# Scores from two fp32r parts in 64-row tiles, two heads at a time, and the weighing of a step in two halves

## The reference

```python
x = attention(ln32(x, ln1), ln32(x, ln1), Wq1, Wkv1, Wo1, bo1) + x   # 16 heads, 16 of q and k per head
x = attention(ln32(x, ln2), context, Wq2, Wkv2, Wo2, bo2) + x
x = geglu_ff(ln32(x, ln3), Wff1, bff1, Wff2, bff2) + x
# then one attention of a single head over the context, a residual and an RMS norm
```

## Time and profile before

| | |
|---|---|
| median of three runs | 856.02 us (854.88 to 858.06) |
| span of the profiled execution | 851.5 us; no other time of that execution is given |
| TensorE busy | 732.0 us, 86%, granted clock 0.945 of 2.4 GHz on average |
| VectorE busy | 575.9 us, 68% |
| ScalarE busy | 471.2 us, 55% |
| POOL busy | 70.4 us, 8% |
| DMA | 49.70 MB, 36645 packets |

### The profile page before, as it was taken

One profiled execution on the slowest core, in us unless ns is written; L12 is line 12 of the kernel. 1 busy time (PEld: TensorE's weight loads), 2 busy tenths in 40 slices (PEclk: granted clock), 3 DMA queues, 4 the chain that ended last, 5 costly groups with the idle time before them and its releaser, 6 DMA issues.

```text
span 851.5 us, 12530 instructions
## 1 busy us (share of the span) xinstructions
PE 732.0 (86%) x4064; PEld 365.9 (43%) x4064; DVE 575.9 (68%) x1030; ACT 471.2 (55%) x918; POOL 70.4 (8%) x63
## 2 busy tenths in 40 slices
PE   0885979999999999999999996647788899999991
PEld 0552522222222222222222343423454688888881
DVE  7783958888888787878888363735557595343357
ACT  0451327777777777777777863025556533332265
POOL 8311100000000000000000020320001011000003
PEclk9998969999999999999999999668889999999995
DMA  8165760030303012030300002222210000000002
GB/s 273 62 219 178 181 246 1 13 89 2 96 3 78 22 40 60 1 99 1 87 14 1 2 19 87 78 78 79 76 39 2 1 1 1 1 1 1 1 1 99
DMA packets 36645, 49.70 MB, mean 58 GB/s; under 512 B 4792, under 2 KB 29688, under 8 KB 35576
## 3 DMA queue, kind: packets, MB, share of 16 engines
q1 hardware_dynamic: 36216, 48.65, 19.0%
q0 software_dynamic: 384, 0.47, 0.3%
HBM read 32.76 MB, written 15.97 MB: 57 GB/s over the span
## 4 chain that ended last, share of the span: by engine, by line
PE 61%; DMA 13%; DVE 9%; SPq 7%; ACT 5%; issue 4%; ACTq 0%; DVEq 0%
PE ps L797 12%; PE ps L784 12%; PE ps L659 10%; SPq L398 6%; DMA stack<-mT 5%; DMA stack<-q_parts 4%; PE ps L958 4%; PE ps L959 3%; PE ps L960 3%; PE ps L633 3%; DMA k_parts<-probs 2%; PE ps L752 2%; PE ps L619 2%; PE ps L974 2%; PE ps L973 1%
## 5 line engine op out<-in xcount | busy, mean ns | idle before, releaser
L1441 DVE TENSOR_REDUCE mm<-ps 128x1 f32<-128x1024 f32 x256 | 301.8, 1219 | 75.5 <-PE ps L659 74.4
L1166 ACT ACTIVATE probs<-ps 128x512 f32<-128x512 f32 x512 | 282.3, 597 | 105.6 <-PE ps L784 102.2
L784 PE MATMUL ps<-stack 99*128 99x512 bf16 x512 | 178.9, 388 | 10.5 <-ACT probs L1166 5.8
L659 PE MATMUL ps<-stack 96*128 96x512 bf16 x512 | 156.5, 386 | 14.6 <-DMA stack<-q_parts 11.7
L797 PE MATMUL ps<-probs,v 128*32 128x512 f32 x1024 | 137.2, 608 | 0.0
L784 PEld LDWEIGHTS ps<-stack 99*128 99x128 bf16 x512 | 42.5, 97 | 191.4 <-ACT probs L1166 173.6
L659 PEld LDWEIGHTS ps<-stack 96*128 96x128 bf16 x512 | 48.7, 99 | 70.9 <-DVE mm L1441 17.7
L551 POOL TENSOR_TENSOR x<-x,rows 128x1024 f32<-128x1024 f32 x12 | 28.3, 2360 | 614.6 <-DVE tok L1411 614.6
L1678 DVE SCALAR_TENSOR_TENSOR k<-ps,cols,early 128x512 f32<-128x512 f32 x32 | 24.0, 750 | 70.1 <-PE ps L960 65.8
L1292 ACT ACTIVATE early<-ps,cols 128x512 f32<-128x512 f32 x32 | 22.1, 690 | 88.3 <-PE ps L960 88.3
L1237 ACT ACTIVATE probs<-ps 96x512 f32<-96x512 f32 x64 | 37.2, 595 | 41.7 <-PE ps L883 41.4
(11 more groups left out here) (142 smaller groups left out, 924.3 us busy)
## 6 DMA issues: line engine op xcount, KB each, us to landing
stack<-q_parts SPq DMA_DIRECT2D x32, 192.0 KB
v_groups<-early SPq DMA_DIRECT2D x8, 512.0 KB, 4.4
stack<-q_parts SPq DMA_DIRECT2D x32, 128.0 KB
v<-v_groups SPq DMA_DIRECT2D x8, 512.0 KB, 13.2
q_parts<-probs SPq DMA_DIRECT2D x8, 384.0 KB, 4.4
k_parts<-probs SPq DMA_DIRECT2D x8, 384.0 KB, 3.0
stack<-k_parts SPq DMA_DIRECT2D x8, 384.0 KB, 4.7
q_parts<-early SPq DMA_DIRECT2D x8, 384.0 KB, 2.6
```

The costliest lines, as they stand in the source:

```text
L659: mm_ = eng.matmul(ps[:, 2 * i + kh, :], qs[0:ROWS, slot, half, h, P * (t0 + i):P * (t0 + i) + P], stack[0:ROWS, 2 + slot, h, BLK * kh:BLK ...
L784: eng.matmul(ps[:, st_bank(g, k, h), :], stack[0:KROWS, 2 + slot, h, P * kc:P * kc + P], qs[0:KROWS, slot, half, h, :], start=True, stop=T ...
L1166: eng.activation(probs[:, k % 2, h, :], ps[:, st_bank(g, k, h), :], ACT.Exp, scale=SCALE).then_inc(exp_done, 1)
L1441: eng.tensor_reduce(mm[:, half, k:k + 1], ps[:, 2 * i:2 * i + 2, :], AX.XY, ALU.max).then_inc(s_red, 1)
```

## The change

Scores come from two fp32r parts instead of three bf16 parts: three products (hi x hi, lo x hi, hi x lo), 3 x 16 = 48 rows, and two more rows for the maximum's two parts. Two heads lie above each other in the two 64-row halves of the array (`HT = 2` tiles, `HP = 2` heads in each). Parts are 4 bytes wide instead of 2, two instead of three; the ring has 4 slots. `middle` and `low` are gone, as are two of four steps of `split_max`. The weighing of a step is issued as two halves of 256 columns. The first score tile of a pair lies in rows 64 and up, the second in rows 0 and up. The heads of a step are taken in the order 0, 2, 1, 3, where 0 and 1 lie in the lower tile and 2 and 3 in the upper. In cross-attention two query tiles of four heads are computed into two banks and reduced by one instruction.

```diff
-PARTS = 3
-RING = 5
-ROWS = 6 * DH
+TILE_ROWS, HT = 64, 2
+HP = HG // HT
+PARTS = 2
+RING = 4
+ROWS = 3 * DH
-Q_PART = (0, 0, 0, 1, 1, 2)
-K_PART = (0, 1, 2, 0, 1, 0)
-RUNS = PARTS
+Q_RUNS = ((0, 2), (2, 1))
+K_RUNS = ((0, 1), (1, 2))
+RUNS = HT * len(Q_RUNS)
+HEADS = (0, 2, 1, 3)
...
-        stack = sb("stack", [P, 4, HG, S], BF16)
+        stack = sb("stack", [P, 4, HP, S], F32R)
...
-            def load_stack(dst, src, heads, which, done):
-
-                i = 0
-                while i < PAIRS:
-                    rise = int(i + 1 < PAIRS and which[i + 1] > which[i])
-                    n = 1
-                    while i + n < PAIRS and which[i + n] == which[i] + rise * n:
-                        n += 1
-                    rows = src[which[i]:which[i] + (n if rise else 1)].rearrange("i (r h) n -> (i r) h n", r=DH)
-                    rows = rows[:, heads, :].rearrange("r h n -> r (h n)")
-                    if not rise:
-                        rows = rows.unsqueeze(0).to_broadcast([n, DH, rows.shape[-1]])
-                    eng.dma_start(dst[DH * i:DH * (i + n), :, :].rearrange("r h n -> r (h n)"), rows).then_inc(done, 16)
-                    i += n
+            def load_stack(dst, src, gg, runs, done):
+
+                for tile in range(HT):
+                    at = HG * gg + HP * tile
+                    for i, n in runs:
+                        rows = src[0:n].rearrange("i (r h) n -> (i r) h n", r=DH)[:, at:at + HP, :]
+                        row = TILE_ROWS * tile + DH * i
+                        eng.dma_start(dst[row:row + DH * n, :, :].bitcast(F32).rearrange("r h n -> r (h n)"),
+                                      rows.rearrange("r h n -> r (h n)")).then_inc(done, 16)
...
-                eng.dma_start(qs[MROW:KROWS, slot, half, :, :].rearrange("i h n -> i (h n)"),
-                              mT[0:PARTS * HG * TPB, half, :]).then_inc(m_in[half], 16)
+                n = PARTS * HP * TPB
+                for tile in range(HT):
+                    eng.dma_start(qs[max_rows(tile), slot, half, :, :].bitcast(F32).rearrange("i h n -> i (h n)"),
+                                  mT[n * tile:n * tile + n, half, :]).then_inc(m_in[half], 16)
...
-            for t in (ident, identb):
-                alone(eng.memset(t[:, :], 0.0))
...
-            alone(eng.memset(stack[MROW:MROW + PARTS, 2:4, :, :], 1.0))
-            alone(eng.memset(k2[:, :, :, :], 0.0))
-            alone(eng.memset(k2[MROW:MROW + PARTS, :, :, 0:CTX], 1.0))
+            upper = [slice(TILE_ROWS * tile + 32, TILE_ROWS * tile + 64) for tile in range(HT)]
+            for half in upper:
+                alone(eng.memset(stack[half, 2:4, :, :].bitcast(F32), 1.0))
+            alone(eng.memset(k2[:, :, :, :, :].bitcast(F32), 0.0))
+            for half in upper:
+                alone(eng.memset(k2[half, :, :, :, 0:CTX].bitcast(F32), 1.0))
...
+                    rows_i = rows_of(1 - i, ROWS)
                     for kh in range(2):
-                        mm_ = eng.matmul(ps[:, 2 * i + kh, :], qs[0:ROWS, slot, half, h, P * (t0 + i):P * (t0 + i) + P],
-                                         stack[0:ROWS, 2 + slot, h, BLK * kh:BLK * kh + BLK], start=True, stop=True)
+                        mm_ = eng.matmul(ps[:, 2 * i + kh, :], qs[rows_i, slot, half, q, P * t:P * t + P],
+                                         stack[rows_i, 2 + slot, q, BLK * kh:BLK * kh + BLK], start=True, stop=True)
...
-                eng.matmul(ps[:, st_bank(g, k, h), :], stack[0:KROWS, 2 + slot, h, P * kc:P * kc + P],
-                           qs[0:KROWS, slot, half, h, :], start=True, stop=True).then_inc(st_full, 1)
+                tile, q = divmod(HEADS[h], HP)
+                eng.matmul(ps[:, st_bank(g, k, h), :], stack[rows_of(tile, KROWS), 2 + slot, q, P * kc:P * kc + P],
+                           qs[rows_of(tile, KROWS), slot, half, q, :], start=True, stop=True).then_inc(st_full, 1)
...
+                cut = slice(BLK // 2 * part, BLK // 2 * part + BLK // 2)
                 for h in range(HG):
-                    mm_ = eng.matmul(ps[32 * h:32 * h + 32, PV, :], v1[:, slot, kc, 32 * h:32 * h + 32],
-                                     probs[:, k % 2, h, :], start=(kc == 0), stop=(kc == KC - 1))
-                mm_.then_inc(pv_done, 1)
+                    mm_ = eng.matmul(ps[32 * h:32 * h + 32, PV, cut], v1[:, slot, kc, 32 * h:32 * h + 32],
+                                     probs[:, k % 2, h, cut], start=(kc == 0 and part == 0), stop=(kc == KC - 1),
+                                     skip_group_check=True)
+                if part == 1:
+                    mm_.then_inc(pv_done, 1)
...
-                for h, n in enumerate((3, 1, 0, 0)):
+                for h in range(HG):
                     scores_t(g, k, h, first)
-                    for _ in range(n):
-                        next(four, None)
-                    if h == 2 and k > 0:
-                        weigh(g, k - 1)
-                    elif h == 2 and not first:
-                        weigh(before(g), 15)
+                    if h % 2 == 0:
+                        for _ in range(2):
+                            next(four, None)
+                    elif k > 0:
+                        weigh(g, k - 1, h // 2)
+                    elif not first:
+                        weigh(before(g), 15, h // 2)
...
-            def middle(u):
-                eng.wait_ge(rest_done, u + 1)
-                eng.activation(part(u)[:, 1, :], rest[:, u % 2, 0:width(u)], ACT.Copy).then_inc(mid_done, 1)
...
-            def low(u):
-                n = width(u)
-                eng.wait_ge(mid_done, u + 1)
-                eng.wait_ge(rest_done, u + 1)
-                eng.tensor_tensor(part(u)[:, 2, :], rest[:, u % 2, 0:n], part(u)[:, 1, :],
-                                  ALU.subtract).then_inc(lo_done, 1)
```

More of the change, by code:

```diff
@@ L405, in of @@
                     return d[bass.ds(pair, 1)].rearrange("o i p n -> (o i) p n")
-                heads = slice(HG * slot, HG * slot + HG)
-                load_stack(stack[:, 2 + slot, :, :], of(k_d), heads, K_PART, k_in[slot])
+                load_stack(stack[:, 2 + slot, :, :], of(k_d), slot, K_RUNS, k_in[slot])
                 for h in range(2):
-                    load_stack(qs[:, slot, h, :, :], of(q_d[h]), heads, Q_PART, q_in[h][slot])
+                    load_stack(qs[:, slot, h, :, :], of(q_d[h]), slot, Q_RUNS, q_in[h][slot])
             def load_v(g):
@@ L859, in _, with scores_2 @@
             self_group((LAST_PAIR, 1), lead=False, chain=chain(0, 0))
-            weigh((LAST_PAIR, 1), 15)
+            for part in range(2):
+                weigh((LAST_PAIR, 1), 15, part)
             eng.wait_ge(att_done, EARLY + 2 * GROUPS - 1)
             turn_out(2 * GROUPS - 1, 1, 2 * GROUPS)
-            def scores_2(G, t):
+            def scores_2(G, m):
                 b, slot = G // GPB, Q2_SLOT[G % 4]
-                if t % TPB == 0:
-                    eng.wait_ge(q2_in[t // TPB][G % 4], 16 * RUNS * (G // 4 + 1))
-                n = KC * G + t
-                if n >= 2:
-                    eng.wait_ge(s2_red, n - 1)
-                for h in range(HG):
-                    mm_ = eng.matmul(ps[:, n % 2, CTX * h:CTX * h + CTX], qs[0:ROWS, slot, t // TPB, h, P * (t % TPB):P * (t % TPB) + P],
-                                     k2[0:ROWS, b, HG * (G % GPB) + h, 0:CTX], start=True, stop=True)
+                half, t0 = divmod(2 * m, TPB)
+                if t0 == 0:
+                    eng.wait_ge(q2_in[half][G % 4], 16 * RUNS * (G // 4 + 1))
+                n = KC // 2 * G + m
+                if n >= 1:
+                    eng.wait_ge(s2_red, n)
+                for q in range(HP):
+                    for t in (t0, t0 + 1):
+                        c = CTXE * (2 * q + t - t0)
+                        for tile in range(HT):
+                            mm_ = eng.matmul(ps[:, tile, c:c + CTXE], qs[rows_of(tile, ROWS), slot, half, q, P * t:P * t + P],
+                                             k2[rows_of(tile, ROWS), b, G % GPB, q, 0:CTXE], start=True, stop=True)
                 mm_.then_inc(s2_full, 1)
@@ L880, in scores_t2 @@
                 if n == 0:
[L881 removed]
+                    eng.wait_ge(m2_in[G % 4], 16 * HT * (G // 4 + 1))
                 eng.wait_ge(exp_done, 64 * GROUPS + UNITS * G + n - 1)
[L883 to L884 removed]
+                tile, q = divmod(HEADS[h], HP)
+                eng.matmul(ps[0:CTXP, ST + h % 2, :], k2[rows_of(tile, KROWS), b, G % GPB, q, :],
+                           qs[rows_of(tile, KROWS), Q2_SLOT[G % 4], half, q, :], start=True, stop=True).then_inc(st_full, 1)
             def weigh_2(G, half):
@@ L1086, in _ @@
                         high(u)
-                    for u in range(PROJ_B0, PROJ_K2):
-                        middle(u)
                 for i in range(TPB):
@@ L1141, in chain @@
                 u = PROJ_2 + 2 * NC * b
-                first = u
```

(2 more changed lines are left out.)

184 lines of the change are left out of this document (83 added, 101 removed).

## The result

| | before | after |
|---|---|---|
| median of four runs each | 857.04 us (854.88 to 858.13) | 1120.01 us (1117.43 to 1122.23) |
| ratio, 95% interval | | 1.308, 1.304 to 1.312 |
| span of the profiled execution | 851.5 | 1119.9 |
| mean granted clock | 0.945 | 0.662 |

The prediction was 789 us, with a range up to 846. The page of the kernel after tells why in one row: PEclk, the granted clock in 40 slices of 28 us, in tenths.

What follows compares the result with a forecast made beforehand. TensorE was taken to set the pace in self-attention, with DMA waits outside the steps. Terms -4 - 12 - 16 - 1 - 23 - 11 = -67 on the 851.5 span gave 784.5; plus 4.5, 789 us, range 762 to 846.

Steps and rivals of the forecast that it cites:

- Six slots: Self-attention step: score matmuls take three slots a half step, 0.69 us, if two row tiles run side by side.
- The first steps ran at half clock after the wait for loads: -2.5: Start of self-attention: half clock there was tied to the wait for loads and would go, saving 2.5 us.
- The form of a step: Self-attention step: score matmuls of different tiles start almost together, four in three slots, with 0.23 lost at changes of shape.
- rival A: Self-attention: the two row tiles don't run side by side, +57 us, total 846; chance 0.12.
- D: Self-attention: fp32r in a 64-row tile streams at fp32's pace, 0.43 a slot, +150 us, total 939; chance 0.04.
- C: Self-attention: weights of the same tile load in the open, +29 us, total 818; chance 0.05.
- The size of a step: Self-attention: a step takes 2.78 us against 2.88, which is -11 us over 111 full steps.
- Loads: Query and key loads without broadcasts: more DMA engines work, share near 0.9, issue 2.3 us a half.
- B: Setup, cross-attention, late q: loads don't get wider or another wait replaces them, +33 us, total 822; chance 0.10.
- Start: Kernel start: POOL memsets release VectorE's three first small operations earlier, -4 us.
- Rest of setup: Setup up to the first scores_t of self-attention: shorter projections, earlier q and key store, -12 us.
- Cross-attention: Start -23 us from faster query loads, with 23 us of VectorE work; groups -11 us from fewer waits and full clock.

Runs made afterwards that it cites:

- e3: Kernel before with the weighing of a step split into two halves of 256 columns, as in the kernel after: 883.32 us.
- e7: Kernel before with self-attention score matmuls contracting rows 0 to 79 only: 856.59 us.
- e10: Kernel before with self-attention score matmuls contracting rows 0 to 63 only: 1041.3 us.
- e11: Kernel before with self-attention score matmuls contracting rows 0 to 65 only: 891.0 us.
- e1: Kernel after with the weighing of a step whole again, behind the fourth scores_t: 952.64 us.
- e2: Kernel after with self-attention score matmuls contracting all 64 rows of their tile instead of 48 and 50: 951.01 us.
- e4: Kernel before, bf16, with self-attention score matmuls contracting rows 0 to 47 only: 944.71 us.
- e5: Kernel after with one burst of 32 fp32 matmuls of 128 rows added in the fourth self-attention step: 1059.3 us, ratio 1.2375.
- e8: The kernel of e1 run again, in four executions: 885.48, 934.38, 955.32 and 935.02 us.
- e9: Kernel after with the burst of e5 also in the first step of each loop pass and behind the loop: 898.8 us, ratio 1.056.
- e12: Kernel before with only self-attention's query loads issued without broadcast: 838.51 us, ratio 0.981.
- e6: Kernel before with only the query loads of self- and cross-attention issued without broadcast: 804.37 us, ratio 0.943.

## Why the prediction was wrong

The step that failed is the one that was never written as a step: "Six slots", "two passes of 256 columns 0.43" and all the rest of the self step were priced at 2.4 GHz, and "The first steps ran at half clock after the wait for loads: -2.5" took the fall at the way in for a cost of the wait, which would go with it. No rival had the clock in it. The runs showed in its place that the fall at the way in does not hang on a long wait. Before, e3, e7, e10 and e11 have one of 3.0 to 5.7 us there. The kernel after, e1, e2, e4, e5, e8, e9 and e12 have none over 0.6 and fall too; of all kernels only e6 doesn't fall. What sets the fall off is not shown. And after that fall, with at most 66 rows in a score matmul and nothing added to the stream, the return took from 48 us to all of the stage. The term: 628 us at 1.2 GHz instead of 2.4, 628 x (1 - 2.94 / 5.17) = +271, where the whole of self-attention is +270.8. That these agree to 1 us is luck in part: the longer step (+7) and the pauses (+4) are in the stage too, so what is left of the forecast gains must have made up for them. e9 gives 221 us back by lifting the clock.

The Trainium skill, TensorE: Matmul & The Clock Gate, section "Part 1: The HAM clock gate (the "warmup" mystery)", says that the default state of TensorE's clock is the throttled one and that activity releases it. The trace does not agree if a full timeline counts as activity: 624 busy us of 628 at 0.50.

Point by point:

- **The form of a step: right.** The two of a pair start together (229.439 and 229.442 in e5), so rival A falls. fp32r slots are 0.235 at 2.4 GHz, so D's mechanism falls. That D alone had forecast a slower kernel, with slots of 0.43, is luck: the slots of the kernel after are 0.427, by the clock and not by the type. Of the matmuls that follow in the same tile the second of each half step takes 0.235, so C falls as it was put, for all four (its term, 4 x 0.06 x 125, is 30 and not 29); the first is the 0.342 of the next point.
- **The size of a step: 0.16 too low.** 2.94 at 2.4 GHz. The first slot behind a weighing is 0.342, so 0.11 over a slot instead of 0.06 (that it is a weight load is the prediction's reading), and from the weighing to the next score matmul it is 0.57 instead of 0.54; the way in is 0.092 instead of 0.10. With 2.94 against 2.88 the term of -11 over 111 steps is +7. The gain of the change in self-attention, forecast at 16, is none at either clock.
- **Loads: right in kind.** The eight halves of the cross start are issued in 15.80 us where they took 32.89, 2.0 a half where 2.3 had been forecast; the DMA share beside them is 0.63 and not near 0.9, but three times the 0.21 of before; the gap before the first early scores is 2.87 instead of 8.98 and they start at 59.4 instead of 72.7. e6 shows the full worth of this: 50 us. B falls. One reading was loose: the k load is three runs of 48, 32 and 16 rows, and not one of 48.

```profile
783.00:795.00 12.00, 9.87 (x66) 7.93 (x67) 7.18 (x26) 2.06 (x4) 0.00 (x0) 1.00 0.63 181
784.31 15.80 SPq L401 DMA_DIRECT2D stack<-q_parts  x32
```

- **Start:** the first transposes begin at 15.4 instead of 20.7, 5.3 earlier (forecast 4).
- **Rest of setup:** -2.4 instead of -12. The early scores start 13.3 us earlier, but from them to the first `scores_t` it is 49.5 instead of 43.9; of this stretch 16 us are at 1.2 GHz (59.4 to 75.8), against 3 before.
- **Cross-attention:** the start gained 14.9, much as e6 (15.5), and not 23. The q loads no longer end it: their issues are over at 800.1, and the first max loads are issued at 809.55 only. Until then VectorE works on norms and maxima, with waits of up to 4.1 us for TensorE between them, where the forecast had put its 23 us of work end to end. The groups lost 19.4 where e6, with loads as wide and the matmuls of before, won 17.7; the granted clock is 0.64 against 0.98 there. So what else the change did there, with the clock, took 37 us; how much of it is the clock alone was not tried.
- **Splitting the weighing:** the extra changes of shape were in the sum; the pauses at the loop ends (1.7 us at 299.6 and 2.0 at 473.0 in the kernel after, up to 4.1 in e9) were not. They cost little by themselves and much where the clock falls at them and stays down, as in e5.

## To carry to other kernels

Price a stream of matmuls at both levels of the clock, and when a change cuts the rows that a matmul contracts, look for where the trace already falls to 1.2 GHz: that short fall may become the whole stage, as it did here. A stage can have two times for the same instructions, so compare the granted clock before anything else. Take the parts of a change apart: here the loads alone were worth 50 us, and the kernel that has the new arithmetic too is 316 slower than that one.

## What the runs showed of the hardware

- TensorE stayed at 1.2 GHz for 628 us in a stream that kept it busy 99% of the time; the mean clock of all four executions is 0.662 to 0.665. The same stream, once at 2.4 GHz, kept it for 106 us (e5), until a pause of 2.8 us.
- Some 5 us of fp32 matmuls of 128 rows (e5; also 5 us in e9) brought 2.4 GHz back; the moment of an unaided return differs between executions of one kernel (153.6 and 326.4 us, times from 885 to 955).
- At pauses of 3 to 4 us inside the stage a stream of 96 rows was back within 7 us (e3), full tiles of 64 rows side by side in 10 us (e2, where the fall at the way in, with a wait of 0.55 only, took 212).
- A loop whose step has one more piece gained a pause of 0.9 to 4.1 us at the end of each pass on TensorE, put down to "issue" (e3 3.86 and 3.29, e9 4.09 and 4.03, e5 2.80 and 0.92), where before, e1 and e6 have no gap over 1 us. With it the queue for instructions brings 16 KB packets within the loop (8 from 303 to 473 us in the kernel after), where it brings none after the first pass with the shorter body. That one causes the other was not tried.
